# A fused Perceiver, recurrent and mixture-of-experts layer on one core: self-attention scores and values computed batch by batch instead of on pairs of batches, and the first cross-attention queries placed ahead of two of their four transposes

## The chip, the cores and the metric

The program runs on one core of a Trainium2 chip. The metric is the device time in microseconds of one execution. Before the change the median of 3 runs is 996.56 us (996.30 to 997.54). One further execution was profiled; its own time is 995.63 us, and the span that the profile covers is 993.8 us.

## The reference

The input `x` has 16 batches of 64 tokens with 512 features (1024 tokens). A second input `context` has 16 batches of 1601 rows. Three blocks follow one another; the change lies in the first lines of the first one.

```
z = self_attn(x, Wq1, Wk1, Wv1)         # 16 batches of 64 x 64 scores
x = layer_norm(x + z, ln1_g, ln1_b)
z = cross_attn(x, context, Wq2, Wk2, Wv2)
...
def self_attn(x, Wq, Wk, Wv):
    Q, K, V = (x @ Wq, x @ Wk, x @ Wv)
    energy = einsum('bqd,bkd->bqk', Q, K)
    lengths = sum(energy[:, 0] != 0)                   # keys whose score with query 0 isn't 0
    energy = where(pad | causal, -inf, energy)
    score = softmax(energy / sqrt(DK))
    return einsum('bqk,bkd->bqd', score, V)
```

Behind it come a feed-forward, a recurrent block and 8 experts, all untouched.

## The kernel before

Tokens lie in 8 tiles of 128 rows (`NT` = 8), so a tile holds two batches of `S` = 64 tokens. Features lie in 4 chunks of 128 (`DC` = 4). There is no scheduler: each engine has one instruction stream written out by hand, and they meet in semaphores. PSUM has 8 banks of 128x512 numbers. `dense_groups()` lists the uses of the banks in order, and the n-th use has bank n mod 8; `wait_bank_free` makes TensorE wait until the use before has been read out, `wait_filled` makes the reader wait for TensorE, and `wait_evacuated` makes anyone wait for the reader.

The stages around the change, with the group names of `dense_groups()`, in the order of TensorE:
- `m1`, `t0`, `gt`: the product of Wq1 and Wk1, the transposed tokens `h1T` (split by ScalarE, L1041, and VectorE, L1378, into a high and a low part in the rounded fp32 type), and gT, their product. It stands at L488.
- `e` (L534): the scores. For each of the 8 tiles, 4 matmuls of 128x128 by 128x128, plain fp32: all 128 queries of two batches against all 128 keys. Half of that is scores between different batches, and VectorE masks it with `own` and `cmask` (L1404, L1405).
- `v` and `len`: the values of 8 tiles (L488, 12 matmuls of 512 columns each), and between them two small products that spread the lengths. VectorE does the softmax meanwhile (L1409 to L1424).
- `pt` (L561): 8 transposes of the 128x128 probabilities `sP`, which ScalarE copies to `sT` (L1030).
- `z` (L482, called with 512 columns): 8 matmuls, `sT` of a tile by its values `vv`.
- `m2` (L488): the product of Wq2 and Wk2.
- `t1` (L495): the first four of the eight tiles, normalised, are transposed, which needs VectorE to have added `z` (L1440) and to have done the layer norm of each (L1333 to L1338, L1350, L1354). ScalarE copies them to `h2T`.
- `q` (L482, 256 columns): the queries of tokens 0 to 255, which need tiles 0 and 1 of `h2T` alone; 16 matmuls. Then come the cross-attention `scores(0)` (L627), `second_queries` of tokens 256 to 511, `late_transposes` (L594), and a loop over 16 batches.

`scores(n)` uses column halves: its stationary operands are 128x64, and two matmuls write partitions 0 to 63 and 64 to 127 of a PSUM bank. `PIECES` cuts its columns into a first piece of 512 and 512 and a second of 321 and 256, and the matmuls alternate between the halves. Before its second piece may start, VectorE must have run `clear_pad(0)` (L1477), which stands in VectorE's stream behind all of its layer norm.

SyncE starts the transfer of context batch 0 when all `v` groups are filled, that of batch 1 when all `z` groups are filled, and further ones as `scores` and `values` of earlier batches end.

Of the kernel before, what the change touches and what calls it, by code (L numbers as in the profile page):

```python
# [69 lines left out]

def bank_uses():

    places = [(name, n % 8) for n, name in enumerate(dense_groups())]
    behind_q = places.index((("q", DC - 1), DC - 1)) + 1
# [27 lines left out]
def perceiver_program(nc, a, out):  # L102
    with ExitStack() as ctx:
# [116 lines left out]
        wq2T, wk2T, gT = at(13312, DC, D), at(15360, DC, D), at(27712, DC, T)  # L220
        wv1, sP, vv = at(31808, DC, D), at(33856, NT, P), at(17408, NT, D)
        m2 = at(35344, DC, D)
# [4 lines left out]
        late2T = [lnw[:, 0, :], lnw[:, 1, :], at(37904, 512), at(38416, 512)]  # L227
        ne, pad, sT = at(6656, NT, P), at(7680, NT, P), at(8704, NT, P)
        own, cmask, kidx_self, sel = (at(12800 + k * P, P) for k in range(4))
        zeros = at(33856, D)  # L230
# [137 lines left out]
        def _(sp):  # L368
# [7 lines left out]
            for e in range(DC):  # L376
# [3 lines left out]
                if e == 1:  # L380
                    load(ident[:], a["ident"], ident_in)
            for t, name in ((own, "own"), (cmask, "cmask"), (kidx_self, "kidx_self"),
                            (sel, "sel"), (tri[:], "tri"), (ones[:], "ones"), (convw[:], "convw"), (fc1b[:], "fc1b"),
                            (convb[:], "convb"), (bgate[:], "bgate"), (fbase[:], "fbase"), (gwT[:], "gwT"),
                            (slot_at[:], "slot_at"), (eidx[:], "eidx"), (kidx[:], "kidx"),
                            (first_rows[:], "first_rows"), (swap[:], "swap"), (sides[:], "sides")):
                load(t, a[name], consts_in)
# [89 lines left out]
        def _(pe):  # L477
# [60 lines left out]
            pe.wait_ge(consts_in, 16 * 18)  # L538

# [16 lines left out]
            for i in range(3, NT):  # L556
                value_tile(i)
            for i in range(NT):
                pe.wait_ge(sa_prob, i // 4 + 1)
                wait_bank_free(pe, "pt", i)  # L560
                signals_filled(nc.tensor.transpose(bank("pt", i)[:, 0:P], sP[:, i, :], ident[:]), "pt", i)  # L561
            for i in range(NT):
                wait_evacuated(pe, "pt", i)
                wait_evacuated(pe, "v", i)
                product(("z", i), 512, [(sT[:, i, :], vv[:, i, :])])
            for c in range(DC):
# [5 lines left out]
                signals_filled(mm, "m2", c)  # L572
            for i in range(4):
                pe.wait_ge(ln_norm[1], before[1] + i + 1)
                transpose_rows(("t1", i), hr[:, i, :])
            for c in range(DC):
                wait_evacuated(pe, "m2", c)
            for i in range(4):
# [6 lines left out]
            def second_queries(c):  # L585
                product(("qh", c), 256, [(m2[:, d, tok(c)], h2T[:, d, 256:512]) for d in range(DC)])

# [439 lines left out]
        def _(act):  # L1027
# [33 lines left out]
            for i in range(NT):  # L1061
# [4 lines left out]
                if i in (3, 4):  # L1066
                    self_exp(i - 3)
            for i in range(NT):
                copy_out(sT[:, i, :], bank("pt", i)[:, 0:P], ("pt", i))
            for c in range(DC):  # L1070
                copy_out(m2[:, c, :], bank("m2", c), ("m2", c))
            for i in range(4):
                transposed_out("t1", i, h2T)
            act.wait_ge(lac_step, 2)
            nc.scalar.activation(lac[:, 1, :], lac[:, 0, :], ACT.Exp).then_inc(lac_done, 1)
            for c in range(DC):
                copy_out(qT[:, c, 0:256], bank("q", c)[:, 0:256], ("q", c))

# [248 lines left out]
        def _(dve):  # L1327
# [28 lines left out]
            def bc(col):  # L1356
                return col.unsqueeze(2).to_broadcast([P, 4, P])

            def mask4(m):
                return m.unsqueeze(1).to_broadcast([P, 4, P])  # L1360

# [12 lines left out]
            for h in range(2):  # L1374
                for i in range(4 * h, 4 * h + 4):
                    t = slice(i * P, (i + 1) * P)
                    dve.wait_ge(first_high, DC + i + 1)
                    V.tensor_tensor(h1T[1][:, :, t], bank("t0", i).rearrange("p (c t) -> p c t", t=P),  # L1378
                                    h1T[0][:, :, t].bitcast(F32), ALU.subtract).then_inc(first_low, 1)
                for i in range(4, 4 + 4 * h):  # L1380
# [7 lines left out]

            dve.wait_ge(consts_in, 16 * 18)
            steps = [0]  # L1390
# [8 lines left out]
            for h in range(2):  # L1399
                e4 = bank("e", h).rearrange("p (q k) -> p q k", k=P)  # L1400
# [42 lines left out]

            for i in range(NT):
                residual("z", i, hr[:, i, :])
                norm_stats(1, i, hr[:, i, :])
                if 1 <= i < 5:
                    norm_gain(1, i - 1, hr[:, i - 1, :], lnw[:, 1, :])
            for i in range(4, NT):
                norm_gain(1, i, hr[:, i, :], lnw[:, 1, :])  # L1450

# [709 lines left out]
```

## Time and profile before

| what | value |
|---|---|
| median of 3 runs | 996.56 us |
| profiled execution, its own time | 995.63 us |
| its span | 993.8 us |
| TensorE busy | 981.2 us (99%) |
| VectorE busy | 615.9 us (62%) |
| ScalarE busy | 394.9 us (40%) |
| time from the first score matmul to the first cross-attention score matmul | 46.21 to 105.30 us |

The table gives shares over the whole program. The change touches 60 us of it, so what counts is the order of events in that stretch: who waits for whom at its borders. Times inside the trace are microseconds from the start of the span. One fp32 matmul of the program shows as two records of MATMUL and two of LDWEIGHTS (weight load), one for each pass; a transpose and a matmul of the rounded type show as one.

### The profile page before, as it was taken

What the parts mean: (1) busy time and instruction counts of PE and PEld (TensorE: products, weight loads), DVE (VectorE), ACT (ScalarE), POOL (GpSimd) and SP (SyncE); (2) the same over time, 40 slices, a digit from 0 to 9 for tenths busy, and PEclk for the clock granted to TensorE, in tenths of its full rate; (3) what the DMA queues carried; (4) which work ended last, traced back from release to release, by engine and by line L of the source; (5) the groups of instructions that cost most, each with busy time, mean ns of one, the idle gap of its engine ahead of it and who ended that gap; (6) DMA issues with size and microseconds to landing.
All of it is one profiled execution on the core that took longest, in us unless ns stands there. A gap on an engine that the chain in (4) does not pass through costs nothing.

```text
span 993.8 us, 14490 instructions
## 1 busy us (share of the span) xinstructions
PE 981.2 (99%) x5444; PEld 781.1 (79%) x5444; DVE 615.9 (62%) x1147; ACT 394.9 (40%) x635; POOL 213.6 (21%) x202
## 2 busy tenths in 40 slices
PE   8999999999999999999999999999999999999998
PEld 4886644445454568878888888999999999999997
DVE  6378254344655656896466768777666665666566
ACT  3332222222111243355657542544445445444441
POOL 2052121002000056454422124721000000000051
PEclk9999999999999999999999999999999999999999
DMA  9709789999999922033311100795674756745543
GB/s 309 309 1 384 287 351 419 429 429 425 424 430 424 398 65 64 11 86 109 108 47 32 33 1 7 274 311 188 178 205 160 192 172 185 192 150 181 161 146 134
DMA packets 47016, 208.99 MB, mean 210 GB/s; under 512 B 5808, under 2 KB 16304, under 8 KB 42736
## 3 DMA queue, kind: packets, MB, share of 16 engines
q1 hardware_dynamic: 41312, 190.02, 52.6%
q0 software_dynamic: 5648, 18.22, 5.5%
q8 instruction: 35, 0.57, 0.2%
q14 instruction: 21, 0.17, 0.1%
HBM read 192.10 MB, written 16.12 MB: 210 GB/s over the span
## 4 chain that ended last, share of the span: by engine, by line
PE 89%; DVE 8%; ACT 2%; issue 1%; DMA 0%; SPq 0%; ACTq 0%; DVEq 0%
PE ps L488 56%; PE ps L656 9%; PE ps L627 8%; PE ps L508 2%; PE ps L482 2%; PE ps L637 1%; PE ps L604 1%; PE ps L961 1%; PE ps L660 1%; DVE stats L1333 1%; PE ps L988 1%; ACT w L1267 1%; PE ps L865 1%; DVE w L1863 1%; PE ps L495 1%
## 5 line engine op out<-in xcount | busy, mean ns | idle before, releaser
L488 PE MATMUL ps<-x,w 128*128 128x320 f32 x1536 | 235.6, 309 | 0.0
L488 PEld LDWEIGHTS ps<-x,w 128*128 128x128 f32 x1536 | 228.0, 188 | 0.4
L1863 DVE TENSOR_TENSOR w<-big,w 128x1536 fp32r<-128x1536 f32 x64 | 112.1, 1753 | 78.4 <-ACT w L1267 78.4
L488 PE MATMUL ps<-hsplit,w 128*128 128x320 f32 x672 | 107.8, 309 | 0.2 <-DVE hsplit L1897 0.2
L1267 ACT CAST w<-big 128x1536 fp32r<-128x1536 f32 x64 | 94.6, 1479 | 30.6 <-PE ps L488 26.8
L488 PEld LDWEIGHTS ps<-hsplit,w 128*128 128x128 f32 x672 | 100.8, 188 | 0.5 <-DVE hsplit L1897 0.5
L627 PE MATMUL ps<-big 128*64 128x512 f32 (+2 forms) x512 | 98.2, 499 | 0.0
L488 PE MATMUL ps<-xcT,u 128*128 128x512 f32 x432 | 98.2, 389 | 0.0
L488 PEld LDWEIGHTS ps<-xcT,u 128*128 128x128 f32 x432 | 81.0, 188 | 17.0 <-DVE xcT L1644 0.2
L656 PE MATMUL ps<-big 128*64 128x512 f32 x384 | 86.4, 597 | 0.3
L1289 ACT CAST hsplit<-big 128x320 fp32r<-128x320 f32 x64 | 29.4, 460 | 138.4 <-DVE big L1893 138.4
L627 PEld LDWEIGHTS ps<-big 128*64 128x64 f32 x512 | 45.1, 136 | 48.0 <-issue 40.3
L1983 POOL TENSOR_TENSOR u<-big,u 128x512 fp32r<-128x512 f32 (+1 forms) x40 | 59.5, 1493 | 103.5 <-ACT u L1101 103.5
L2068 POOL DMA_DIRECT2D ys<-big x28 | 16.8, 603 | 270.2 <-DVE big L1885 269.2
L1959 POOL TENSOR_TENSOR rstd<-veps,consts 128x1 f32<-128x1 f32 x48 | 34.0, 711 | 177.0 <-DVE veps L1338 176.6
L488 PE MATMUL ps<-hT,u 128*128 128x512 f32 x288 | 66.1, 390 | 0.8 <-DVE big L1633 0.7
L488 PEld LDWEIGHTS ps<-hT,u 128*128 128x128 f32 x288 | 53.9, 188 | 12.6 <-issue 0.9
L656 PEld LDWEIGHTS ps<-big 128*64 128x64 f32 x384 | 26.1, 137 | 45.3 <-issue 45.1
L1491 DVE COPY big<-ps 128x512 f32<-128x512 f32 x16 | 11.1, 691 | 74.2 <-PE ps L637 74.2
L1030 ACT COPY big<-ps 128x512 f32<-128x512 f32 (+2 forms) x52 | 25.0, 519 | 74.6 <-PE ps L488 47.1
L1897 DVE TENSOR_TENSOR hsplit<-big,hsplit 128x320 fp32r<-128x320 f32 (+1 forms) x72 | 32.1, 455 | 33.7 <-ACT hsplit L1289 33.7
L1105 ACT COPY big<-ps 128x256 f32<-128x256 f32 x16 | 6.0, 372 | 78.8 <-PE ps L637 78.6
(338 smaller groups left out, 1556.0 us busy)
## 6 DMA issues: line engine op xcount, KB each, us to landing
big<-in_ctxT SPq DMA_DIRECT2D x16, 3202.0 KB, 17.7
big<-in_ctx SPq DMA_DIRECT2D x16, 3072.0 KB, 16.9
big<-in_w_units SPq DMA_DIRECT2D x64, 768.0 KB, 4.7
big<-in_dense_units SPq DMA_DIRECT2D x41, 256.0 KB, 2.7
xs<-big POOLq DMA_DIRECT2D x1, 5120.0 KB, 17.3
big<-in_gate_units SPq DMA_DIRECT2D x12, 384.0 KB, 3.0
hr<-xs SPq DMA_DIRECT2D x28, 160.0 KB, 5.8
ys<-big POOLq DMA_DIRECT2D x28, 160.0 KB, 5.7
```

The source lines that it names most:

```text
L482: mm = nc.tensor.matmul(bank(*g)[:, 0:cols], lhsT, rhs, start=(k == 0), stop=(k == len(pairs) - 1))
L488: mm = nc.tensor.matmul(dst, lhs[x], rhs[w], start=start and x + w == 0, stop=stop and x == 1)
L508: mm = nc.tensor.matmul(bank("m1", c), wq1T[:, e, tok(c)], wk1T[:, e, :], start=(e == 0), stop=(e == DC - 1))
L627: mm = nc.tensor.matmul(ps[half * S:half * S + S, 2 + piece, 0:w], qT[:, d, n * S:(n + 1) * S], cT[n % 2][:, d, col:col + w], start=(d == ...
L656: mm = nc.tensor.matmul(ps[half * S:half * S + S, 6, :], pts[:, t, half * S:half * S + S], nat[j][:, narrow * KH + t, :], start=(t == 0), ...
L1030: signals_evacuated(nc.scalar.copy(dst, src_bank), *g)
L1267: nc.scalar.copy(wsplit[f % RING][0][:], wraw[f % RING]).then_inc(w_high, 1)
L1289: nc.scalar.copy(hsplit[f % 2][:, 0:SLOTS], hid[f % 2]).then_inc(hid_high, 1)
L1863: V.tensor_tensor(wsplit[f % RING][1][:], wraw[f % RING], wsplit[f % RING][0][:].bitcast(F32), ALU.subtract).then_inc(w_low, 1)
L1897: V.tensor_tensor(h[:, to:to + hi - lo], hid[f % 2][:, lo:hi], h[:, lo:hi].bitcast(F32), ALU.subtract).then_inc(hid_low, 1)
L1959: G.tensor_tensor(rstd[:, i:i + 1], veps[:, i:i + 1], consts[:, 0:1], ALU.pow).then_inc(ln_rstd[L], 1)
L1983: G.tensor_tensor(low[:, 0:w], unit_raw(u)[:, 0:w], high[:, 0:w].bitcast(F32), ALU.subtract).then_inc(u_low, 1)
```

## The change

- Scores: for each batch alone, a 128x64 stationary operand by 64 moving columns. The even batch of a tile writes partitions 0 to 63 and the odd batch 64 to 127, in 64 columns; so there are 64 matmuls of 64 columns instead of 32 of 128, and the scores between batches are not computed. `own` is gone, and VectorE's masks and softmax work on 64 columns for each tile instead of 128.
- Values: the tokens of two neighbouring tiles are put in another order when `h1T` is split (`value_order`), so that value tile 2k holds in its halves the batches 4k and 4k+2, and 2k+1 the batches 4k+1 and 4k+3. The four 64x64 probability blocks of two tiles lie in one 128x128 block, so there are 4 transposes instead of 8. Each batch's values are then one matmul with 64 rows of keys and 64 columns of queries: a quarter of the array. There are 16 such matmuls of 512 columns instead of 8 on the whole array.
- Order on TensorE: only the transposes of tiles 0 and 1 stand ahead of the first queries; those of tiles 2 and 3 stand behind the second and third query group. ScalarE's copies follow that order, and its exponential for `lac` moves behind the query copies.
- Order on VectorE: the additions of `z` are taken in pairs and ahead of the statistics of later tiles.

```diff
@@ bank_uses / dense_groups
-    g += [("pt", i) for i in range(NT)]
+    places[at_z:at_z] = [(("pt", k), k) for k in range(NT // 2)]
@@ TensorE
                 for q in range(4):
                     for d in range(DC):
-                        mm = nc.tensor.matmul(bank("e", h)[:, q * P:(q + 1) * P], gT[:, d, tok(4 * h + q)],
-                                              hT[:, d, tok(4 * h + q)], start=(d == 0), stop=(d == DC - 1))
+                        for s in range(2):
+                            b = 2 * (4 * h + q) + s
+                            mm = nc.tensor.matmul(bank("e", h)[s * S:s * S + S, q * S:q * S + S], gT[:, d, value_cols(b)],
+                                                  hT[:, d, b * S:b * S + S], start=(d == 0), stop=(d == DC - 1))
...
-            for i in range(NT):
-                wait_evacuated(pe, "pt", i)
-                wait_evacuated(pe, "v", i)
-                product(("z", i), 512, [(sT[:, i, :], vv[:, i, :])])
+            for k in range(NT // 2):
+                wait_evacuated(pe, "pt", k)
+                for i in (2 * k, 2 * k + 1):
+                    wait_evacuated(pe, "v", i)
+                    wait_bank_free(pe, "z", i)
+                for r in range(2):
+                    keys = slice(r * S, r * S + S)
+                    for s in range(2):
+                        own = slice(s * S, s * S + S)
+                        mm = nc.tensor.matmul(bank("z", 2 * k + r)[own, :], sT[keys, k, own], vv[keys, 2 * k + s, :],
+                                              start=True, stop=True)
+                    signals_filled(mm, "z", 2 * k + r)
...
             for c in range(DC):
                 product(("q", c), 256, [(m2[:, d, tok(c)], h2T[:, d, 0:256]) for d in range(DC)])
+                if c in (1, 2):
+                    second_rows_turned(c + 1)
@@ ScalarE
-                    nc.scalar.copy(h1T[0][:, :, i * P:(i + 1) * P],
-                                   bank("t0", i).rearrange("p (c t) -> p c t", t=P)).then_inc(first_high, 1)
+                    nc.scalar.copy(value_order(h1T[0], i), by_batch(bank("t0", i))).then_inc(first_high, 1)
@@ VectorE
-                chained(V.scalar_tensor_tensor(ne[:, hs[h], :], e4, 0.0, mask4(own), ALU.not_equal, ALU.mult))
+                chained(V.tensor_scalar(ne[:, hs[h], :], e4, 0.0, None, ALU.not_equal))
...
+            for i in range(2):
+                attended(i)
+                attended_stats(i)
+            first_gain(0)
+            attended(2, 3)
+            first_gain(1)
+            attended(4, 5)
+            attended_stats(2, 3)
+            first_gain(2, 3)
+            attended(6, 7)
+            attended_stats(4, 5, 6, 7)
+            first_gain(4, 5, 6, 7)
```

TensorE's stream at the values stood so before: `pt` (L561), `z` (L482), then the first of `m2` (L488).

```order
198 L561 MATMUL ps<-ident,big 128x128 x8
199 L482 MATMUL ps<-big 128x512 x8
200 L488 MATMUL ps<-wk2high_63,wq2high_55 128x512
```

With the change it stands so at the scores (first row, L551) and at the values (`pt` L578, `z` L588).

```order
99 L551 MATMUL ps<-big 64x64 x64
...
198 L578 MATMUL ps<-ident,big 128x128 x4
199 L588 MATMUL ps<-big 64x512 x16
200 L503 MATMUL ps<-wk2high_63,wq2high_55 128x512
```

So half of the transposes are gone, and the 8 value matmuls became 16 that write 64 partitions each. Further on, before the change, `t1`, `q` and the first scores of the cross-attention stood so.

```order
248 L495 MATMUL ps<-ident,hr 128x128 x16
249 L482 MATMUL ps<-big 128x256 x16
250 L627 MATMUL ps<-big 64x512 x8
251 L627 MATMUL ps<-big 64x321
252 L627 MATMUL ps<-big 64x256
253 L627 MATMUL ps<-big 64x321
254 L627 MATMUL ps<-big 64x256
```

With the change two tiles (8 transposes) stand ahead of the first 8 query matmuls, and the two others come one by one between the rest.

```order
248 L510 MATMUL ps<-ident,hr 128x128 x8
249 L497 MATMUL ps<-big 128x256 x8
250 L510 MATMUL ps<-ident,hr 128x128 x4
251 L497 MATMUL ps<-big 128x256 x4
252 L510 MATMUL ps<-ident,hr 128x128 x4
253 L497 MATMUL ps<-big 128x256 x4
254 L660 MATMUL ps<-big 64x512 x8
```

On VectorE, the rows from the first gain on stood so before: gain of a tile, then addition and statistics of the next.

```order
74 L1350 SCALAR_TENSOR_TENSOR hr<-hr,mv,lnw 128x512
75 L1354 SCALAR_TENSOR_TENSOR hr<-hr,rstd,lnw 128x512
76 L1440 TENSOR_TENSOR hr<-hr,ps 128x512
77 L1333 BN_STATS stats<-hr 128x6
78 L1335 BN_AGGR mv<-stats 128x2
79 L1338 TENSOR_SCALAR veps<-mv 128x1
```

With the change two additions (L1473) follow each of the two first gains (L1384, L1388), and the next statistics come after them.

```order
74 L1384 SCALAR_TENSOR_TENSOR hr<-hr,mv,lnw 128x512
75 L1388 SCALAR_TENSOR_TENSOR hr<-hr,rstd,lnw 128x512
76 L1473 TENSOR_TENSOR hr<-hr,ps 128x512 x2
77 L1384 SCALAR_TENSOR_TENSOR hr<-hr,mv,lnw 128x512
78 L1388 SCALAR_TENSOR_TENSOR hr<-hr,rstd,lnw 128x512
79 L1473 TENSOR_TENSOR hr<-hr,ps 128x512 x2
80 L1367 BN_STATS stats<-hr 128x6
```

## Rows read from the trace of the kernel before

**Rows 1.** The page: busy time of each engine, and the chain's shares by engine
```profile
PE 981.2 (99%) x5444; PEld 781.1 (79%) x5444; DVE 615.9 (62%) x1147; ACT 394.9 (40%) x635; POOL 213.6 (21%) x202
...
PE 89%; DVE 8%; ACT 2%; issue 1%; DMA 0%; SPq 0%; ACTq 0%; DVEq 0%
```

**Rows 2.** Busy time by stage, stretches cut at the borders of TensorE's stages
```profile
core 0: us, PE busy (x) PEld busy (x) DVE busy (x) ACT busy (x) POOL busy (x), PEclk, DMA share, GB/s
46.21:53.27 7.06, 7.06 (x65) 7.06 (x64) 1.97 (x3) 0.59 (x1) 0.00 (x0) 1.00 0.02 3
...
75.60:76.72 1.12, 1.12 (x9) 0.86 (x8) 0.00 (x0) 0.90 (x4) 0.00 (x0) 1.00 0.00 0
76.72:83.65 6.93, 6.93 (x18) 3.12 (x17) 5.42 (x12) 1.05 (x7) 1.55 (x2) 1.00 1.06 409
83.65:94.81 11.16, 11.16 (x50) 8.96 (x48) 10.66 (x22) 1.77 (x3) 3.49 (x4) 1.00 0.98 418
94.81:98.17 3.36, 2.10 (x17) 1.68 (x16) 3.17 (x8) 2.75 (x6) 1.00 (x3) 1.00 1.08 465
98.17:105.30 7.13, 7.13 (x34) 6.02 (x35) 5.14 (x8) 1.12 (x3) 0.55 (x1) 1.00 1.01 433
105.30:108.75 3.45, 3.45 (x19) 1.17 (x20) 0.11 (x1) 0.37 (x1) 0.00 (x0) 1.00 0.85 354
108.75:111.00 2.25, 2.25 (x19) 1.34 (x15) 0.00 (x0) 0.00 (x0) 0.00 (x0) 1.00 0.06 17
```

**Rows 3.** Small matmuls of the router (L825), 601 to 603 us: durations, starts
```profile
L825 PE MATMUL ps<-gwT,big x8: 170/256/256, 601.3 to 602.0; 128*128 128x8 f32 x8
```

**Rows 4.** Cross-attention scores of batch 0 (L627): weight loads in time
```profile
105.24 0.20 PEld L627 LDWEIGHTS ps<-big 128*64 128x64 f32 x4 [0.33 <-issue]
105.73 0.14 PEld L627 LDWEIGHTS ps<-big 128*64 128x64 f32 x2 [0.28 <-issue]
```

**Rows 5.** The same scores, matmul groups that ran within 108.78 to 110.32
```profile
L627 PE MATMUL ps<-big 128*64 128x256 f32 x8 | 1.9, 379 | 0.0
L627 PE MATMUL ps<-big 128*64 128x321 f32 x6 | 1.8, 433 | 0.0
```

**Rows 6.** Timeline around the end of the values, all engines
```profile
75.82 1.94 ACT L1030 COPY big<-ps 128x512 f32<-128x512 f32 x9 [2.13 <-PE ps L488]
75.88 0.34 SPq L370 DMA_DIRECT2D big<-in_ctxT  x1
...
77.95 0.69 DVE L1440 TENSOR_TENSOR hr<-hr,ps 128x512 f32<-128x512 f32 x1 [4.73 <-PE ps L482]
```

**Rows 7.** Timeline between `m2` and the first queries
```profile
96.67 0.63 PE L495 MATMUL ps<-ident,hr 128*128 128x128 f32 x4 [0.39 <-DVE hr L1440]
...
97.33 0.59 ACT L1030 COPY big<-ps 128x512 f32<-128x512 f32 x1 [0.27 <-PE ps L495]
...
98.17 0.45 PE L482 MATMUL ps<-big 128*128 128x256 f32 x1 [0.87 <-ACT big L1030]
```

**Rows 8.** VectorE in time: last softmax step, last gain, memset, first count
```profile
72.25 0.69 DVE L1424 TENSOR_TENSOR big<-big,rinv 128x512 f32<-128x512 f32 x1
...
102.70 0.75 DVE L1354 SCALAR_TENSOR_TENSOR hr<-hr,rstd,lnw 128x512 f32<-128x512 f32 x1
105.81 0.11 DVE L1477 MEMSET ps<- 64x65 f32 x1 [2.36 <-ACT big L1030]
```

**Rows 9.** VectorE splits the first four tiles of transposed tokens
```profile
21.63 2.47 DVE L1378 TENSOR_TENSOR h1Tlow<-ps,h1Thigh 128x512 fp32r<-128x512 f32 x4
```

**Rows 10.** Context transfers: issue times on SyncE's queue, and sizes
```profile
83.92 0.33 SPq L370 DMA_DIRECT2D big<-in_ctxT  x1
...
111.10 15.14 SPq L370 DMA_DIRECT2D big<-in_ctxT  x2
...
big<-in_ctxT SPq DMA_DIRECT2D x16, 3202.0 KB, 17.7
big<-in_ctx SPq DMA_DIRECT2D x16, 3072.0 KB, 16.9
```

More of the change, by code:

```diff
@@ L73, in bank_uses @@
     places = [(name, n % 8) for n, name in enumerate(dense_groups())]
+    at_z = places.index((("z", 0), 0))
+    places[at_z:at_z] = [(("pt", k), k) for k in range(NT // 2)]
     behind_q = places.index((("q", DC - 1), DC - 1)) + 1
@@ L220, in perceiver_program @@
         wq2T, wk2T, gT = at(13312, DC, D), at(15360, DC, D), at(27712, DC, T)
-        wv1, sP, vv = at(31808, DC, D), at(33856, NT, P), at(17408, NT, D)
+        wv1, sP, sP_flat, vv = at(31808, DC, D), at(33856, NT, S), at(33856, NT * S), at(17408, NT, D)
         m2 = at(35344, DC, D)
@@ L227, in perceiver_program, with value_cols, value_order, by_batch @@
         late2T = [lnw[:, 0, :], lnw[:, 1, :], at(37904, 512), at(38416, 512)]
-        ne, pad, sT = at(6656, NT, P), at(7680, NT, P), at(8704, NT, P)
-        own, cmask, kidx_self, sel = (at(12800 + k * P, P) for k in range(4))
+        ne, pad, sT = at(6656, NT, S), at(7680, NT, S), at(8704, NT // 2, P)
+        cmask, kidx_self, sel = at(12800, S), at(12928, S), at(13056, P)
+        def value_cols(b):
+            c = (b // 4 * 2 + b % 2) * P + b % 4 // 2 * S
+            return slice(c, c + S)
+        def value_order(part, i):
+            pair = part[:, :, i // 2 * 2 * P:(i // 2 + 1) * 2 * P]
+            return pair.rearrange("p c (s r q) -> p c s r q", s=2, r=2)[:, :, :, i % 2, :]
+        def by_batch(rows):
+            return rows.rearrange("p (c s q) -> p c s q", s=2, q=S)
         zeros = at(33856, D)
@@ L381, in _ @@
                     load(ident[:], a["ident"], ident_in)
-            for t, name in ((own, "own"), (cmask, "cmask"), (kidx_self, "kidx_self"),
+            for t, name in ((cmask, "cmask"), (kidx_self, "kidx_self"),
                             (sel, "sel"), (tri[:], "tri"), (ones[:], "ones"), (convw[:], "convw"), (fc1b[:], "fc1b"),
@@ L557, in _ @@
                 value_tile(i)
-            for i in range(NT):
[L559 to L562, printed above, removed]
-                wait_evacuated(pe, "pt", i)
-                wait_evacuated(pe, "v", i)
-                product(("z", i), 512, [(sT[:, i, :], vv[:, i, :])])
+            for k in range(NT // 2):
+                pe.wait_ge(sa_prob, k // 2 + 1)
+                wait_bank_free(pe, "pt", k)
+                signals_filled(nc.tensor.transpose(bank("pt", k)[:, 0:P], sP_flat[:, k * P:(k + 1) * P], ident[:]), "pt", k)
+            for k in range(NT // 2):
+                wait_evacuated(pe, "pt", k)
[9 more added lines that the diff above has]
+                    signals_filled(mm, "z", 2 * k + r)
             for c in range(DC):
@@ L572, in _, with second_rows_turned @@
                 signals_filled(mm, "m2", c)
-            for i in range(4):
+            def second_rows_turned(i):
                 pe.wait_ge(ln_norm[1], before[1] + i + 1)
                 transpose_rows(("t1", i), hr[:, i, :])
+            second_rows_turned(0)
+            second_rows_turned(1)
             for c in range(DC):
                 wait_evacuated(pe, "m2", c)
-            for i in range(4):
+            for i in range(2):
                 wait_evacuated(pe, "t1", i)
@@ L585, in second_queries @@
             def second_queries(c):
+                if c == 0:
+                    for i in (2, 3):
+                        wait_evacuated(pe, "t1", i)
                 product(("qh", c), 256, [(m2[:, d, tok(c)], h2T[:, d, 256:512]) for d in range(DC)])
@@ L1067, in _ @@
                     self_exp(i - 3)
-            for i in range(NT):
-                copy_out(sT[:, i, :], bank("pt", i)[:, 0:P], ("pt", i))
+            for k in range(NT // 2):
+                copy_out(sT[:, k, :], bank("pt", k)[:, 0:P], ("pt", k))
             for c in range(DC):
                 copy_out(m2[:, c, :], bank("m2", c), ("m2", c))
-            for i in range(4):
-                transposed_out("t1", i, h2T)
+            transposed_out("t1", 0, h2T)
+            transposed_out("t1", 1, h2T)
+            for c in range(DC):
+                copy_out(qT[:, c, 0:256], bank("q", c)[:, 0:256], ("q", c))
+                if c in (1, 2):
+                    transposed_out("t1", c + 1, h2T)
             act.wait_ge(lac_step, 2)
             nc.scalar.activation(lac[:, 1, :], lac[:, 0, :], ACT.Exp).then_inc(lac_done, 1)
-            for c in range(DC):
-                copy_out(qT[:, c, 0:256], bank("q", c)[:, 0:256], ("q", c))
             def second_queries_out(c):
@@ L1356, in bc @@
             def bc(col):
-                return col.unsqueeze(2).to_broadcast([P, 4, P])
+                return col.unsqueeze(2).to_broadcast([P, 4, S])
             def mask4(m):
-                return m.unsqueeze(1).to_broadcast([P, 4, P])
+                return m.unsqueeze(1).to_broadcast([P, 4, S])
             for i in range(NT):
@@ L1375, in _ @@
                 for i in range(4 * h, 4 * h + 4):
-                    t = slice(i * P, (i + 1) * P)
                     dve.wait_ge(first_high, DC + i + 1)
-                    V.tensor_tensor(h1T[1][:, :, t], bank("t0", i).rearrange("p (c t) -> p c t", t=P),
-                                    h1T[0][:, :, t].bitcast(F32), ALU.subtract).then_inc(first_low, 1)
+                    V.tensor_tensor(value_order(h1T[1], i), by_batch(bank("t0", i)),
+                                    value_order(h1T[0], i).bitcast(F32), ALU.subtract).then_inc(first_low, 1)
                 for i in range(4, 4 + 4 * h):
@@ L1386, in _ @@
                                 ALU.subtract).then_inc(first_low, 1)
-            dve.wait_ge(consts_in, 16 * 18)
+            dve.wait_ge(consts_in, 16 * 17)
             steps = [0]
@@ L1399, in _ @@
             for h in range(2):
-                e4 = bank("e", h).rearrange("p (q k) -> p q k", k=P)
+                e4 = bank("e", h)[:, 0:4 * S].rearrange("p (q k) -> p q k", k=S)
                 wait_filled(dve, "e", h)
@@ L1442, in residual, with attended, first_gain, attended_stats @@
                 wait_evacuated(dve, name, i)
[L1444 to L1450, printed above, removed]
+            def attended(*tiles):
+                for i in tiles:
+                    residual("z", i, hr[:, i, :])
+            def first_gain(*tiles):
+                for i in tiles:
+                    norm_gain(1, i, hr[:, i, :], lnw[:, 1, :])
+            def attended_stats(*tiles):
+                for i in tiles:
+                    norm_stats(1, i, hr[:, i, :])
+            for i in range(2):
+                attended(i)
[9 more added lines that the diff above has]
+            first_gain(4, 5, 6, 7)
             def decay_start():
@@ L2107 @@
     rows, keys = np.arange(P)[:, None], np.arange(P)[None, :]
-    same = (rows // S) == (keys // S)
     t_of = (np.arange(NT)[None, :, None] * P + np.arange(P)[:, None, None])
@@ L2141 @@
                for w in (v["L0_ffn_down_proj_w"].transpose(0, 2, 1),)], axis=2),
-        "ident": np.eye(P, dtype=f), "own": same.astype(f),
-        "cmask": np.where(same & (keys <= rows), f(0), f(NEG)), "kidx_self": np.broadcast_to(keys % S, (P, P)).astype(f),
+        "ident": np.eye(P, dtype=f),
+        "cmask": np.where(keys[:, 0:S] <= rows % S, f(0), f(NEG)), "kidx_self": np.broadcast_to(keys[:, 0:S], (P, S)).astype(f),
         "sel": (rows == (keys // S) * S).astype(f), "tri": (rows <= keys).astype(f), "ones": np.ones((P, P), f),
```

2 lines of the change are left out of this document (1 added, 1 removed).

## Prediction

> **What bounds the kernel now.** I read the page first, for the busy shares and for the chain of work that ended last. TensorE is busy 99% of the span, and the chain runs over it for 89% [rows 1]; what is taken from TensorE's stream is therefore gained, as long as nothing it waits for is late instead. The shares say nothing of single stages, so I read next the busy time by stretches, cut where TensorE goes from one stage to the next [rows 2]: after the bounds of the stretch come the busy time and the count of records of each engine. TensorE fills the scores (7.06 us), the transposes (1.12), the values (6.93) and `m2` (11.16). Ahead of the first queries it is busy 2.10 of 3.36 us: 1.26 us idle. The timeline there [rows 7] shows 0.39 us of it waiting for VectorE and 0.87 us for ScalarE's copy. VectorE is busy 10.66 of 11.16 us beside `m2` [rows 2]; from its first addition at 77.95 [rows 6] to the end of its last gain at 103.45 [rows 8] it has 25.5 us of work nearly without a hole. So there are two chains side by side: TensorE's, and VectorE's layer norm, which ends 1.85 us ahead of the first cross-attention scores at 105.30.
>
> **The scores.** There are now 32 matmuls, 64 records, in 7.06 us: 0.110 us each [rows 2], with weight loads busy the whole time. The router's matmuls with 8 columns and the same 128x128 weights start 8 in about 0.8 us (601.32, and the 8th at 602.0), 0.10 us apart [rows 3]; so at this size loading 128 columns of weights and streaming 128 columns of fp32 each take about 0.1 us and lie over one another. The change halves both and doubles the records to 128, in two column halves. Do the halves run side by side? The cross-attention scores use them: 16 records of 512 columns take 3.45 us, 0.43 for a pair [rows 2], as much as one record of 512 columns of the values on the whole array (6.93 / 16 = 0.433). Their weight loads go in pairs too: two take 0.14 us, four 0.20, so a further pair costs 0.06 [rows 4]. I take 0.057 us for a pair, between half of 0.110 and 0.06. The rest of 108.75 to 111.00, 2.25 - 8 x 321/512 x 0.433 = 0.08 us, is the cost of leaving this mode; with the entry I take 0.2 for a stage. Scores: 64 x 0.057 + 0.2 = 3.85 us, a gain of 3.2. Bounds, since no row has such short work in halves: 64 x 0.055 = 3.5 below; above, every record after the other, 128 x 0.055 + 0.2 = 7.25 if the load and the stream set the pace, and 128 x 0.110 + 0.2 = 14.3 if 0.1 us is a price for each record whatever its width. Pairs of loads in 0.06 speak against the last.
>
> The Trainium skill (TensorEngine Tiling (Array Packing), Performance Considerations) speaks against this edit: a matmul carries some 60 cycles of overhead, and a dimension already small shouldn't be what tiling lives on. By its figure, an estimate of 0.025 us at 2.4 GHz on top of each pair would make this stage 64 x 0.082 + 0.2 = 5.4 us and the gain 1.6. The trace before has no row with such short streams, so no run here shows it yet.
>
> VectorE's masks and softmax come with it. They are off the path: the last softmax step ends at 72.94, and TensorE asks for it at 75.60 [rows 2, 8]. All of it moves 3.2 us earlier with the scores and has half the columns. If nothing of it shrank it would still end ahead.
>
> **The value order.** The split of `h1T` is on the path (four VectorE operations in 2.47 us from 21.63, and then `gt` starts) [rows 9]. It writes runs of 64 numbers instead of 128, with the same count; already now it writes 4 separate runs. I take 0, and 0.3 us for eight pieces as the upper bound (an eighth more on 2.47).
>
> **The transposes.** Four of eight go, half of 1.12 us [rows 2]. But ScalarE's nine copies start at 75.82 with that of the last value tile; nine take 1.94 us [rows 6], of which the long one is about 0.5 and a short one 0.18. The first `sT` is ready at about 76.5, and the values need it; they started at 76.72. TensorE will wait where it transposed. Gain 0.
>
> **The values.** Before: 8 matmuls, 16 records of 512 columns, 6.93 us. Now 16 matmuls, 32 records, on quarters. If all four quarters run at once, two tiles take two passes, 0.87 us, and the stage 4 x 0.87 + 0.2 = 3.66 us: a gain of 3.3. No row shows halves of the key rows side by side; column halves are shown [rows 2]. Bounds: 3.5 below; 7.1 if only column halves overlap; all one after another would be 13.9, which the column halves exclude. I take 3.66, because the two halves of the keys read other partitions and write other banks, and because column halves go their own way: between 108.78 and 110.32 all 8 narrow records had run, but only 6 of the 8 wide ones [rows 5], though the program has them in turn, wide first. A quarter doesn't wait for its predecessor in another quarter, if that holds for rows also.
>
> **The order at the queries.** Before, from the end of `m2` to the end of the queries: 3.36 + 7.13 = 10.49 us. Now: transposes of two tiles (2 x 0.44: 8 records of 128 columns at the 0.11 us that the scores show), then ScalarE's copy of the second (from the end of the last transposes at 97.11 to the first query at 98.17: 1.06 us [rows 7]), 7.13 of queries, and 2 x 0.44 of transposes inside: 9.95. Gain 0.54. These transposes need gains 2 and 3 of VectorE, which are long done by then: a tile costs 25.5 / 8 = 3.19 us, of which an addition is about 0.7 [rows 6], a gain two operations of 0.75 with overlap, 1.45 [rows 8], and the statistics the rest, 1.0. In the new order six additions, four statistics and four gains end 14.3 us after its start, and the transposes come some 20 us after it.
>
> **What could be late next.** VectorE's chain starts 1.2 us after the values, as now, so it moves with the scores only: 77.95 - 3.2 + 0.1 for the entry of the mode = 74.85, and ends at 100.35. `clear_pad(0)` must have run ahead of the second piece of scores(0). TensorE reaches scores(0) at 105.30 - 7.0 = 98.3 and the second piece 3.45 later, 101.75: 1.3 us of slack, where it was 5. Context transfers: the first two batches are 4 x about 3.1 MB = 13.4 MB [rows 10]; at the 418 GB/s beside `m2` [rows 2] they take 32 us from 72.7 on and end at 104.7. The first scores need batch 0, there at about 88.7, and scores(1) starts at about 113. The following transfers start on TensorE's events, so they move with it. Nothing behind changes, and the gain is carried to the end.
>
> **Sum.** 3.2 + 0 + 3.3 + 0.5 = 7.0 us. The profiled execution took 995.63, so 988.6; the median of the runs is 0.93 higher, so 989.5 is the forecast.
>
> **The rivals.**
> A, the forecast, 989.5: chance 0.60.
> B, the quarters of the values don't overlap by four. Each matmul is two passes on the same quarter; if starts keep to program order, only the second pass of one and the first of the next overlap: 17 x 0.433 + 0.2 = 7.6 us, a loss of 0.6 instead of a gain of 3.3, so 993.4. If only row halves fail to overlap, 7.1 and 992.9. For it: no row of quarters. Against: rows 5. Chance 0.17. The Trainium skill (TensorE: Matmul & The Clock Gate, Part 3) has the rule: matmuls start and end strictly in program order. The 8 against 6 of rows 5 disagree with it for column halves.
> C, the short scores in halves gain nothing, because loads of the halves take turns or each pair pays an overhead: 7.25 us at worst, so 992.9; an overhead in between gives 989.5 to 992.9. Chance 0.11.
> D, B and C together: 996.5, no change. Chance 0.03.
> E, slower: 0.110 us is a price of every record. Then 128 of them take 14.3 us, a loss of 7.2, and with 3.3 and 0.5 gained elsewhere the kernel is 3.4 us slower: 999.9. It decides from 0.085 us a record on (3.8 us gained elsewhere, spread over 128 records, on top of 0.055). Chance 0.05.
> F, VectorE's chain becomes the bound: it loses 1 to 2 us of the gain, 990.5 to 991.5. Chance 0.04.
>
> **How the numbers follow.** A measurement of this kernel can tell 0.2%, 2 us, from no change. Faster: A, B, C and F, less a little for small gains: 0.90. Same: D and what of B and C ends worse: 0.05. Slower: 0.05. The range reaches from 988.3 (the scores at their lower bound 3.5, values at 3.5, half of the transposes gained) to 993.5, which takes in B, C and F and leaves out D and E, and the spread of the runs.
>
> **What would show it.** In the profile after: the score records 128 in about 3.9 us, in pairs; the value records 32 in about 3.7 us; TensorE idle ahead of the values about 0.4 us, waiting for ScalarE; `m2` starting at about 77.2; the first queries 1.9 us after `m2`; no wait for the memset; scores(0) at about 98.3. The forecast is wrong if the score records stand over 0.08 apart, if the value stage takes over 7 us, or if TensorE waits inside scores(0).

## The result and the profile after

The changed kernel takes 989.46 us (median of 4 runs, 989.03 to 989.60) against 996.43 us before (4 runs, 995.71 to 997.54): a ratio of 0.993, 95% interval 0.9918 to 0.9941, so 7.0 us less. The forecast was 989.5. The profiled execution took 989.58 us, its span 987.9.

The page of the changed kernel: busy time by engine. TensorE has 7.2 us less to do than in [rows 1], though it has 76 records more.

```profile
PE 974.0 (99%) x5520; PEld 775.5 (79%) x5520; DVE 612.0 (62%) x1147; ACT 393.7 (40%) x631; POOL 210.7 (21%) x202
```

The same stretches of TensorE's stages as in [rows 2], in the same columns: scores, transposes, values, `m2`, the way to the first queries, and the queries with the transposes of two tiles inside.

```profile
core 0: us, PE busy (x) PEld busy (x) DVE busy (x) ACT busy (x) POOL busy (x), PEclk, DMA share, GB/s
47.34:51.22 3.88, 3.88 (x129) 3.81 (x129) 1.18 (x3) 0.59 (x1) 0.00 (x0) 1.00 0.02 6
73.54:74.81 1.27, 0.60 (x6) 0.39 (x4) 0.00 (x0) 1.07 (x5) 0.00 (x0) 1.00 0.50 121
74.81:78.47 3.66, 3.66 (x33) 1.37 (x33) 2.31 (x5) 0.19 (x2) 0.48 (x1) 1.00 0.94 350
78.47:89.66 11.19, 11.19 (x49) 9.00 (x49) 10.70 (x21) 1.76 (x3) 2.60 (x4) 1.00 1.00 430
89.66:91.69 2.03, 1.05 (x9) 0.82 (x8) 1.96 (x4) 1.56 (x3) 0.00 (x0) 1.00 0.92 381
91.69:99.70 8.01, 8.01 (x42) 6.81 (x43) 7.63 (x18) 2.29 (x5) 2.63 (x4) 1.00 1.03 444
```

The scores went from 7.06 to 3.88 us, the values from 6.93 to 3.66. The stretch of the transposes got longer by 0.15, since TensorE waits for ScalarE now. From the end of `m2` to the end of the queries it is 10.04 instead of 10.49. That is 6.75 us in sum, less 0.03 on `m2`. From the first cross-attention scores to the end of the span it is 888.2 us, and was 888.5, so nothing behind gives the gain back.

The timeline of the changed kernel, ahead of the values and in them, shows the wait and how the quarters run.

```profile
73.54 0.60 PE L578 MATMUL ps<-ident,big 128*128 128x128 f32 x4
73.74 1.26 ACT L1063 COPY big<-ps 128x512 f32<-128x512 f32 x5 [2.14 <-PE ps L503]
...
74.78 0.24 PEld L588 LDWEIGHTS ps<-big 64*64 64x64 f32 x8 [0.88 <-ACT big L1063]
74.81 1.52 PE L588 MATMUL ps<-big 64*64 64x512 f32 x12 [0.67 <-ACT big L1063]
75.26 0.18 PEld L588 LDWEIGHTS ps<-big 64*64 64x64 f32 x4 [0.25 <-issue]
75.69 0.18 PEld L588 LDWEIGHTS ps<-big 64*64 64x64 f32 x4 [0.25 <-issue]
76.02 0.69 DVE L1473 TENSOR_TENSOR hr<-hr,ps 128x512 f32<-128x512 f32 x1 [7.27 <-PE ps L588]
```

Weight loads come by four every 0.43 us, the length of one record of 512 columns: all four quarters stream at once. VectorE starts at 76.02, 1.21 us after the first value matmul, much as in [rows 6] (1.23).

TensorE's wait ahead of the values is for ScalarE's second copy, not for the first. The edit takes the tiles in pairs and asks for the banks of both value tiles before the first matmul of the pair; the second of these banks is the one that holds the second transpose. In the trace ScalarE's first copy of the probabilities ends at 74.49 and its second at 74.66, and the values start 0.15 us after the second. Before the change they started 0.14 us after the first (76.58, then 76.72). This is read from the trace and the program; no run takes the second wait away by itself.

At the other end of the stretch VectorE's last gain and its memset stand so (the order of [rows 8]).

```profile
100.78 0.75 DVE L1388 SCALAR_TENSOR_TENSOR hr<-hr,rstd,lnw 128x512 f32<-128x512 f32 x1
101.62 0.11 DVE L1527 MEMSET ps<- 64x65 f32 x1
```

The memset is over at 101.73. The second piece of scores(0) starts 3.45 us after 99.70, at 103.15: TensorE doesn't wait.

In the profiled executions the stretch moved by 5.6 us only (first cross-attention scores at 99.7 instead of 105.3), because the scores began at 47.34 instead of 46.21. The first tokens landed later: VectorE's first statistics start at 7.63 us in this profile and at 6.41 in that of before. That isn't the change. In the eleven profiles of the experiments below the first statistics start between 6.5 and 8.0 us, in the two whose kernel begins like that of before too (7.68 and 7.28). The profile of before was an early one, and its own time lay 0.93 us under the median of its runs.

### The profile page after: what moved, and what is told of

It reads as the page before. It is cut to its first block, busy times and chain, and to the rows that moved or that the text cites. A ratio compares the mean times of both kernels' runs of the same rounds, so it can differ in the third digit from the quotient of the medians.

```text
span 987.9 us, 14637 instructions
## 1 busy us (share of the span) xinstructions
PE 974.0 (99%) x5520; PEld 775.5 (79%) x5520; DVE 612.0 (62%) x1147; ACT 393.7 (40%) x631; POOL 210.7 (21%) x202
## 4 chain that ended last, share of the span: by engine, by line
PE 92%; DVE 5%; DMA 1%; ACT 1%; issue 0%; SPq 0%; POOL 0%; ACTq 0%; DVEq 0%
PE ps L503 62%; PE ps L689 9%; PE ps L660 8%; PE ps L670 1%; PE ps L497 1%; PE ps L637 1%; PE ps L994 1%; PE ps L693 1%; PE ps L1021 1%; DVE stats L1367 1%; PE ps L898 1%; PE ps L510 1%; DMA xr<-in_x 1%; PE ps L702 1%; DVE hr L1376 1%; PE ps L858 1%
```

## The experiments

All times are medians. Each set of runs was made on one chip, with runs of the kernel before between them; the sets ran on different chips, and the kernel before had a median of 996.3 to 996.7 us in each. A difference of a few tenths between two sets therefore means little, and the stretches of the traces decide there. Each profile is one execution, whose start differs, so a stretch below goes from one event of TensorE to a later one of the same trace.

### The scores alone

The kernel before, with this edit at L534:

```diff
-  mm = matmul(bank("e", h)[:, q*P:(q+1)*P], gT[:, d, tok(4*h+q)], hT[:, d, tok(4*h+q)], ...)
+  for s in range(2):
+      own_cols = slice((4*h+q)*P + s*S, (4*h+q)*P + (s+1)*S)
+      mm = matmul(bank("e", h)[s*S:s*S+S, q*P+s*S:q*P+(s+1)*S], gT[:, d, own_cols], hT[:, d, own_cols], ...)
```

> The kernel before, with the scores alone in column halves (64 matmuls of 64 columns; the blocks between batches are not computed, the masks stay as they are). Theory: the two halves run side by side and nothing behind is late, so the score records (L534) take 3.9 us instead of 7.06 and all behind moves 3.2 us ahead: 993.2 us against 996.4. Rival (each record has a price of its own): 7 us or more for the stage and no gain. The stage's own length in the profile decides, whatever the start of the run does.

993.55 us, ratio 0.9967 (0.9955 to 0.9979), against an expected 993.2. The chain of this run has the stage in one piece:

```profile
47.30 3.88 PE ps L536 x128
```

The halves run side by side at this size too, 0.06 us a pair. Of the 3.2 us that the stage gives, 3.0 show in the medians (996.54 to 993.55).

### Two by two: the values and the order

Three kernels undo the order edit in the changed kernel: on all three engines, on VectorE alone, and on TensorE with ScalarE alone. A fourth adds the order edit, but not the values, to the scores-alone kernel.

```diff
 # VectorE, old order
+  for i in range(NT):
+      attended(i)
+      attended_stats(i)
+      if 1 <= i < 5:
+          first_gain(i - 1)
+  first_gain(4, 5, 6, 7)
 # TensorE, old order (ScalarE's copies likewise)
+  for i in range(4):
+      second_rows_turned(i)
...
-      if c in (1, 2):
-          second_rows_turned(c + 1)
```

> The changed kernel with the order edit undone on all three engines: four transposes ahead of all queries, ScalarE's copies so too, VectorE tile by tile. Theory: the values on quarters free TensorE 3.3 us earlier but not VectorE, which starts at the same offset; the fourth transpose waits for the bank that the last addition of z frees, 18.6 us after VectorE's start in the old order, so at 94.6 where m2 ends at 89.7. The queries end 3.6 us later than in the changed kernel: 993.0 us. The order edit is then worth 3.6 us and the values by themselves nearly nothing. Rival, as the prediction's sum had it: the order is worth 0.5 us, 990.0 us, and the values 3.3.

> The changed kernel with VectorE's order alone undone. Theory: the first two gains are in time, but the bank of the second transpose is freed by the addition of z 5, 15.1 us after VectorE's start, 91.1, where TensorE asks at 90.1: 1.0 us later, 990.4 us. Rival: TensorE's order alone carries the whole edit, 989.5.

> The changed kernel with TensorE's and ScalarE's order alone undone (four transposes ahead of all queries). Theory: the last addition of z in the new order ends at 91.6, the fourth transpose comes then, the copy 1.06 us behind it, and the queries end 0.55 us later than in the changed kernel: 990.0 us. Rival: VectorE's order carries nothing and this costs 3.6 us as undoing both, 993.0.

> The kernel before with the scores in column halves and with the order edit on TensorE, ScalarE and VectorE, but with the values on the whole array as before (8 transposes, 8 matmuls). With the run of the scores alone (993.55 us), the one with all orders undone (values but no order, 995.78) and the changed kernel (both, 989.46) it completes a table of two by two. Theory, as in the prediction's sum: by itself the order takes 0.5 us from the wait and the copy ahead of the queries, 993.0 us; the value edit brings its 3.3 us only with the order, so the two are worth more together (4.1) than apart (-2.2 and 0.5). Rival: the order by itself brings nothing or more than 1.5 us.

| kernel (all with the scores in halves) | us | ratio to before |
|---|---|---|
| values on the whole array, old order | 993.55 | 0.9967 (0.9955 to 0.9979) |
| values on the whole array, new order | 992.33 | 0.9960 (0.9947 to 0.9974) |
| values on quarters, old order | 995.78 | 0.9992 (0.9983 to 1.0001) |
| values on quarters, old order of VectorE alone | 992.00 | 0.9953 (0.9939 to 0.9967) |
| values on quarters, old order of TensorE alone | 990.12 | 0.9933 (0.9919 to 0.9946) |
| values on quarters, new order (the change) | 989.46 | 0.9930 (0.9918 to 0.9941) |

With the old order the value edit doesn't gain 3.3 us; the kernel is 2.2 us slower than without it. The theory of that run had 993.0, so 2.8 us were not expected. With the new order the value edit gains 2.9 us (992.33 to 989.46). The order edit by itself gains 1.2. Apart the two are worth -2.2 and 1.2, together 4.1.

From the first transpose behind `m2` to the first cross-attention scores the traces show 9.96 us in the changed kernel, 10.62 with TensorE's order undone (0.7 more, expected 0.55) and 11.09 with VectorE's order undone (1.1 more, expected 1.0). Both undone cost far more than the two apart. TensorE's timeline of the run with all orders undone, from the end of `m2`:

```profile
91.58 0.63 PE L510 MATMUL ps<-ident,hr 128*128 128x128 f32 x4 [1.01 <-DVE hr L1469]
93.31 0.63 PE L510 MATMUL ps<-ident,hr 128*128 128x128 f32 x4 [1.10 <-DVE hr L1469]
95.04 1.09 PE L510 MATMUL ps<-ident,hr 128*128 128x128 f32 x4 [1.10 <-DVE hr L1469]
97.00 9.34 PE L497 MATMUL ps<-big 128*128 128x256 f32 x32 [0.87 <-ACT big L1061]
```

Three waits for VectorE's additions, 3.2 us, and two more groups of transposes ahead of the queries put them at 97.00 where the changed kernel has them at 91.69. Then the same 32 records take 9.34 us instead of the 7.13 of [rows 2]. The stretches of this run say why (busy TensorE, granted clock, DMA):

```profile
78.80:90.00 11.20, 11.20 (x49) 1.00 1.01 434
90.00:95.00 5.00, 1.83 (x13) 0.96 0.98 415
95.00:97.00 2.00, 1.09 (x4) 0.50 0.98 423
97.00:101.30 4.30, 4.30 (x10) 0.50 1.04 448
101.30:106.34 5.04, 5.04 (x25) 0.99 0.93 401
```

After 5 us in which TensorE was busy for 1.83, the granted clock is 0.50 (1.2 instead of 2.4 GHz) for over 6 us. The last group of transposes takes 1.09 us instead of 0.63, and the first 4.3 us of the queries run at half speed and lose 2.2. The run with VectorE's order undone alone was expected at 990.4 and took 992.0. Its profiled execution has no such stretch and took 991.03 us, but three of its five runs report a mean clock of 0.998 and took 992.0 to 992.95. So the clock probably fell in these as well; no trace of them was kept.

### The gaps filled

The kernel with all orders undone, with one matmul of 512 fp32 columns, which nobody reads, ahead of each of the three waiting transpose groups:

```diff
+            wait_bank_free(pe, "q", 0)
             for i in range(4):
+                if i:
+                    nc.tensor.matmul(bank("q", 0), ident[:], xr[:, 0, :], start=True, stop=True)
                 second_rows_turned(i)
```

> The kernel with all orders undone, plus three matmuls of 512 fp32 columns (0.86 us each) whose result nobody reads, one ahead of each transpose group that waits for VectorE. They lie inside waits of 1.0 to 1.1 us. Theory: in the run without them TensorE did 1.8 us of work in 4 us ahead of the queries, its granted clock fell to half, and the queries took 9.3 us instead of 7.1; with the gaps filled the clock stays at full speed, the queries take 7.1 us, and the time is 2.2 us less than without, 993.6 us. Rival (the longer queries come from something else, such as the transfers): 995.8 as without.

993.38 us, ratio 0.9970 (0.9959 to 0.9981), against an expected 993.6. More work for TensorE, and 2.4 us less time. Its stretches: from the end of `m2` up to the queries, and the queries.

```profile
89.40:95.92 6.52, 5.01 (x23) 1.00 1.01 432
95.92:103.05 7.13, 7.12 (x34) 1.00 1.01 433
```

From the first transpose behind `m2` to the first cross-attention scores it is 13.65 us, where it was 16.30 without the extra matmuls. The 2.7 us between them are the 2.2 of the queries and the 0.5 of the last transposes, so this part of the loss was the clock. What is left is 13.65 against 9.96 in the changed kernel: 3.7 us for the order on all engines, where 3.6 were expected. And with the clock held, the value edit in the old order is worth 0.2 us (993.55 to 993.38): nearly nothing, as the theory had it.

### How the parts of the array take their matmuls

Two kernels write the score matmuls in another sequence, one the value matmuls. The matmuls are the same. In the last one all waits for ScalarE's copies and for banks also come ahead of the first value matmul, so that TensorE idles for 1.84 us there instead of 0.67.

```diff
 # halves in turn by fours
-   for q in range(4):
-       for d in range(DC):
-           for s in range(2):
+   for q in range(4):
+       for s in range(2):
+           for d in range(DC):
 # halves apart by sixteens
+   for s in range(2):
+       for q in range(4):
+           for d in range(DC):
 # quarters apart, for the values
-   for k in range(NT // 2):
-       for r in range(2):
-           for s in range(2):
+   for r in range(2):
+       for s in range(2):
+           for k in range(NT // 2):
```

> The changed kernel with the score matmuls of a tile written half after half: four of the first half, then four of the second, instead of in turn. Theory (each half takes its matmuls from the queue by itself): same stage, 3.9 us, and 989.5 us. Rival (starts keep to program order): four of one half after one another, then four of the other, 7.1 us for the stage and 992.7.

> As the one before, but 16 matmuls (32 records) of one half ahead of the 16 of the other, for four tiles each. Theory: the halves overlap only as far as the queue reaches ahead; if it holds less than 32 records and their weight loads, the stage grows, up to 7.1 us (992.7); if it holds them, 3.9 us plus what the last half has left alone. I expect between 4.5 and 7.1 us. Rival (program order): 7.1 us as in the run before.

> The changed kernel with the value matmuls written quarter after quarter: the four pairs of tiles on one quarter of the array, then the next quarter. Theory: 8 records per quarter, all four side by side if the queue reaches over 32 records: 3.7 to 4.1 us for the stage as now; the first filled bank comes no later than now if quarter (0, 1) starts at once. Time 989.5 to 990. Rival (program order, or a queue that reaches less far): up to 13.9 us for the stage, and up to 10 us slower.

| sequence | stage, us | time, us |
|---|---|---|
| scores, halves alternate (the change) | 3.88 | 989.46 |
| scores, four matmuls of a half, then four | 4.92 | 990.46 |
| scores, sixteen and sixteen | 7.07 | 992.12 |
| values, quarters alternate (the change) | 3.66 | 989.46 |
| values, four matmuls of a quarter after another | 12.28 | 999.16 |

The chains of the three runs show the stages (score records L551, value records L589):

```profile
47.31 4.92 PE ps L551 x128
```

```profile
46.57 7.07 PE ps L551 x128
```

```profile
75.70 12.28 PE ps L589 x32
```

My theory as written down fell for the values, and for the fours of the scores too: sequence does matter. The other theory, strictly one after another in program order, gives 7.1 for the fours and doesn't fit either. What fits all three is a short reach, and the traces show how far it goes. A record doesn't name its half; the spacing of the starts tells them apart. By fours, the first half's eight records start from 47.24 on, and the first one of the second half starts at 47.53, right behind the fifth and ahead of the last three (47.59, 47.64, 47.70). By sixteens, 29 records have started when the other half's first one starts at 48.19, again with three of 32 still to come. With the quarters apart, the second quarter's first record starts at 77.44, right behind the fifth of the first quarter's eight. So a free part overtakes three records, one and a half matmuls, in each of the three runs. How that depends on the matmul's size or type was not measured.

The next part starts beside the fourth record from the end, then, and four steps of each border are shared. For the quarters, with three borders, this leaves 20 steps of 0.43 us out of 32, 8.8 us with 0.2 for entering and leaving. The weight loads of that run show it: one at a time, then by twos and threes.

```profile
77.01 0.13 PEld L589 LDWEIGHTS ps<-big 64*64 64x64 f32 x1 [0.30 <-issue]
77.44 0.19 PEld L589 LDWEIGHTS ps<-big 64*64 64x64 f32 x3 [0.30 <-issue]
77.90 0.34 PEld L589 LDWEIGHTS ps<-big 64*64 64x64 f32 x2 [0.27 <-issue]
78.75 0.34 PEld L589 LDWEIGHTS ps<-big 64*64 64x64 f32 x2 [0.51 <-issue]
```

The 12.28 us that were measured hold a second loss:

```profile
75.70:77.80 2.10, 2.10 (x6) 0.74 (x8) 0.00 (x0) 0.00 (x0) 0.00 (x0) 1.00 0.89 378
77.80:84.70 6.90, 6.90 (x18) 2.29 (x16) 1.72 (x4) 0.00 (x0) 0.56 (x1) 0.51 1.02 440
84.70:87.95 3.25, 3.25 (x13) 0.91 (x9) 1.57 (x4) 0.00 (x0) 0.00 (x0) 1.00 0.98 423
```

The clock was granted at half from 77.8 to 84.7. At full clock those 6.9 us would be 3.4, and the stage 8.8, as the 20 steps give. The one of its eight runs with a clock of 1.00 took 995.69 us. Ahead of the fall TensorE had been idle for 1.84 us and then, from 75.70 to 77.44, had streamed on one quarter alone; while the clock was low it had two quarters at work nearly throughout. Which of the two brought it down, the idle time or the single quarter, no run here separates.

### Two steps further

The changed kernel, with the four transposes of the probabilities and ScalarE's copies of them ahead of the last value tile; and on top of it, the transposes of tile 2 ahead of the first queries.

```diff
-            for i in range(3, NT):
+            for i in range(3, NT - 1):
                 value_tile(i)
             for k in range(NT // 2):
...
+            value_tile(NT - 1)
 # and, for the second kernel
             second_rows_turned(1)
+            second_rows_turned(2)
```

> The changed kernel with the four transposes of the probabilities, and ScalarE's copies of them, ahead of the last value tile. Theory: the 0.67 us in which TensorE waits for ScalarE ahead of the values are gone; the value stage starts 0.1 us after the last value tile instead of 1.27 us, of which 0.44 are the transposes, moved: 0.75 us less, 988.7 us. VectorE's layer norm starts earlier by the same. Rival (VectorE or the transfers of context become late instead): no change, 989.5.

> The kernel with the early transposes of the probabilities, and with the transposes of tile 2 ahead of the first query group instead of behind the second. Theory: TensorE waits there 1.0 us for ScalarE's copy of tile 1; the bank for tile 2 is freed by the addition of z 6, 14.9 us after VectorE's start, so at 89.5, and 0.44 us of transposes fit before the first queries at 90.26: 0.4 us less, 987.7. Rival: the bank comes later than ScalarE's copy and the queries wait, 988.1 or more.

The first takes 988.10 us (987.85 to 988.36), ratio 0.9916 (0.9902 to 0.9929), against an expected 988.7; the intervals overlap, but its slowest run is below the fastest of the changed kernel. From the first record behind the scores to the first of `m2` it is 0.7 us shorter (26.56 instead of 27.25), for the 0.75 expected. The rest of the 1.4 us between the medians is not in these stages; its profile began 0.6 us earlier, and for the medians the cause stays open. Its value stage follows the last value tile without a hole:

```profile
70.71 2.77 PE ps L503 x12
73.47 3.59 PE ps L589 x32
```

The first record on quarters starts 0.32 us behind the last of the value tile, whose records follow each other by 0.23. So the entry to the quarters costs 0.09 us.

The second takes 988.61 us, ratio 0.9922 (0.9908 to 0.9935), where 987.7 was expected: no better by the medians. TensorE waits 0.3 us for the addition that frees the bank (90.22). Even so the way from the first transpose behind `m2` to scores(0) is 9.53 us, where the first of the two kernels has 9.97: the 0.4 us of the theory are there. They are too small for these medians, since the kernel before was itself 0.3 us slower in this set (996.67 against 996.33), and this profile began 0.6 us later.

## Why the prediction was right

- **Scores.** Forecast 3.85 us and a gain of 3.2, measured 3.88 and 3.18. The pairs cost what the loads of [rows 4] said. Rivals C, D and E fell with this row. By the estimate from the 60 cycles of the Trainium skill (TensorEngine Tiling (Array Packing), Performance Considerations) it would have been 5.4 us; here a pair started every 0.058 us, so this case doesn't show such a cost on top of a pair.
- **Values.** Forecast 3.66 us, measured 3.66. B fell. The Trainium skill has a rule of strict order in start and end (TensorE: Matmul & The Clock Gate, Part 3). Taken by whole matmuls, the four at a time of this stage still keep it: the first passes of four matmuls start within 0.02 us of each other, and their second passes 0.45 us later. What breaks it is [rows 5] and the run by fours, where a matmul of the second half starts at 47.53, ahead of the fourth of the first half (47.64). But my own reading of [rows 5], that a half goes its own way, was too wide: the sequences apart show that it does so over three records. The forecast held because this kernel writes the quarters in turn, which the prediction did not ask for; that part of it was luck.
- **Transposes.** Forecast no gain and an idle time of 0.4; measured 0.67 idle and 0.15 us lost. The working had the values wait for the first copy alone. They wait for the second too, since the banks of both value tiles of a pair are asked for first, and the copies start 0.16 us apart.
- **Order.** Forecast 0.54 in the stretch, measured 0.45; by itself, in the run without the value edit, it measured 0.48 in its own profile (10.44 to 9.96, first transpose to first cross-attention scores) and 1.2 by the medians. But the sum put 3.3 to the values and 0.5 to the order as if they were independent. They aren't: without the order the values gain nothing, and the clock falls on top. The working looked at the gains that the transposes need. It left out the banks: the four transposes go to banks that the additions of the last four tiles of `z` free, and in the old order the last of these ends 18.6 us after VectorE's start. My working costed the values with the new order in place, which made the sum right; it named no rival for the pair.
- **What could be late next.** Forecast 1.3 us of slack for the memset, measured 1.4, and F fell with it. The working's 4 x 3.1 MB are 12.4, not 13.4; no number of the forecast hangs on it. The context transfers cost nothing: the stages behind move as one, 888.2 us against 888.5.
- **The split in value order.** Four VectorE operations take 2.48 us as in [rows 9] (2.47). Cost 0, as forecast.
- **The sum.** 7.0 forecast, 6.97 measured by the medians. The stages of the traces give 6.7: 0.15 less for the transposes, 0.1 less for the order. That the medians come within 0.03 us of the forecast is luck; the runs before alone spread over 1.8 us. The profiled executions by themselves differ by 6.1, with 1.1 us of the start between them; to take the stages apart and not the spans was what kept that out.

## What to carry to other kernels

In this case work on column halves or quarters of TensorE overlapped almost fully, even with 64 columns a matmul, when the program alternated between the parts; written block after block, only the last four records of a block had the next one beside them. When a stage is shortened, look at what the next engine does with the time: here VectorE's order had to change with it, and a row of short waits of 3.2 us cost another 2.7 us in clock. Cost such edits as pairs, and ask of each what it is worth without the other.

## What the hardware showed that I had not expected

- The granted clock fell to 0.50 after 5 us with 1.83 us of work (the old order), and three matmuls of no use inside the waits kept it at 1.00 and made the kernel 2.4 us faster.
- It fell also after 1.84 us of idle time and 1.7 us on a single quarter, and then stayed at 0.51 from 77.8 to 84.7 us though TensorE was busy throughout. On four quarters at once, behind 0.67 us of idle time, it stayed at 1.00.
- A free part of the array overtook three records and no more in each of the three runs with blocks. For the same 128 score records it is 3.88 us in turn, 4.92 by fours and 7.07 by sixteens.
- A bank that is asked for early is paid for: waiting for both banks of a pair held TensorE until the second copy, 0.17 us behind the first.
